# Vision block on one core: the weighing of the keys and the fills change places in TensorE's program from the third period on

## The reference

```
h = conv_involution(x)                       # per pixel: 16 hidden channels, relu, 9 filter taps;
                                             # out = sum over 9 taps of shifted x * tap; reshape (4, 4096, 64)
n = layernorm(h)
Q, K, V = n @ Wq + bq, n @ Wk + bk, n @ Wv + bv
h = h + softmax(Q @ K.T / sqrt(64)) @ V      # 4096 queries against 4096 keys, per image
n = layernorm(h)
idx = argmax(n @ router_w.T + router_b)      # one of 32 experts for each of 16384 tokens
t = relu(n @ W1[idx] + b1[idx])              # 64 -> 16
h = h + relu(t @ W2[idx] + b2[idx])          # 16 -> 64
```

## Time and profile before

| what | us |
|---|---|
| median of 3 runs (1106.17 to 1106.96) | 1106.2 |
| the profiled execution, its own time | 1105.74 |
| its span, first to last instruction | 1104.0 |
| TensorE (PE) busy | 1081.4 |
| PE weight loads busy | 531.2 |
| ScalarE busy | 575.2 |
| VectorE busy | 527.7 |
| one pass over 256 keys: scores, start to start of the next work | 1.72 |
| its weighing, likewise | 1.72 |

### The profile page before, as it was taken

The page is one execution under the profiler, slowest core; times in us unless marked ns, Lnnn a source line. Parts: engine busy times, 40 slices in busy tenths (PEclk is TensorE's granted clock), DMA queues, the critical chain, the costliest instruction groups (busy, mean ns, idle before and its releaser), DMA issues.

```text
span 1104.0 us, 28734 instructions
## 1 busy us (share of the span) xinstructions
PE 1081.4 (98%) x12492; PEld 531.2 (48%) x12492; DVE 527.7 (48%) x1039; ACT 575.2 (52%) x649; POOL 13.3 (1%) x44
## 2 busy tenths in 40 slices
PE   7799999999999999999999999999999999999997
PEld 4233333445454555435444454555555555555543
DVE  7888665436064553735546364564423131312305
ACT  2466666546555454645546454554645445464543
POOL 3100000000000000000000000000000000000000
PEclk9899999999999999999999999999999999999999
DMA  4847431113025141222313023240100101010000
GB/s 96 207 120 168 97 72 32 40 39 78 2 68 120 39 109 39 48 68 68 80 40 96 16 70 77 66 82 11 47 7 11 41 12 42 11 42 1 12 1 21
DMA packets 23377, 63.43 MB, mean 57 GB/s; under 512 B 4254, under 2 KB 8702, under 8 KB 22860
## 3 DMA queue, kind: packets, MB, share of 16 engines
q1 hardware_dynamic: 22364, 61.26, 23.3%
q10 hardware_dynamic: 880, 0.23, 0.1%
HBM read 52.87 MB, written 5.47 MB: 53 GB/s over the span
## 4 chain that ended last, share of the span: by engine, by line
PE 95%; DVE 1%; issue 1%; ACT 1%; DMA 1%; ACTq 0%; DVEq 0%; PEld 0%; PEldq 0%; SPq 0%
PE z_ps L787 40%; PE scores L776 38%; PE both L627 5%; PE both L758 4%; PE both L618 2%; PE both L766 1%; PE both L705 1%; PE both L724 1%; PE both L715 1%; DMA filter_ring<-filters 1%; PE both L750 0%; PE scores L627 0%; PE both L674 0%; DVE hres L1160 0%; PE z_ps L758 0%
## 5 line engine op out<-in xcount | busy, mean ns | idle before, releaser
L996 ACT ACTIVATE probs<-scores 128x1024 f32<-128x1024 f32 x512 | 496.4, 1021 | 470.7 <-PE scores L776 470.7
L776 PE MATMUL scores<-g_t,keys_t 64*64 64x512 f32 x4096 | 509.5, 591 | 1.5 <-ACT g_t L975 1.2
L787 PE MATMUL z_ps<-probs,keys 64*64 64x512 f32 x4096 | 506.8, 592 | 0.0
L776 PEld LDWEIGHTS scores<-g_t,keys_t 64*64 64x64 f32 x4096 | 210.9, 134 | 236.1 <-issue 230.1
L787 PEld LDWEIGHTS z_ps<-probs,keys 64*64 64x64 f32 x4096 | 196.4, 133 | 189.5 <-issue 178.6
L1220 DVE SCALAR_TENSOR_TENSOR hidden<-both,chosen 128x1024 f32<-128x1024 f32 x44 | 53.9, 1225 | 198.9 <-PE both L627 193.8
L1160 DVE TENSOR_TENSOR hres<-hres,tap_product 128x504 f32<-128x504 f32 (+1 forms) x128 | 88.1, 688 | 11.1 <-issue 0.9
L1148 DVE SCALAR_TENSOR_TENSOR tap_product<-filter_ring,w,xin 128x504 f32<-128x504 f32 (+1 forms) x117 | 87.0, 743 | 9.2 <-DMA filter_ring<-filters 5.5
L627 PE MATMUL both<-y_t,w 64*64 64x512 f32 x448 | 60.5, 589 | 0.0
L758 PE MATMUL both<-hidden,w 64*64 64x512 f32 x448 | 56.7, 592 | 0.0
L1261 DVE COPY o_sb<-both 128x512 f32<-128x512 f32 x14 | 9.7, 691 | 85.2 <-PE both L758 85.2
(11 more groups left out here) (162 smaller groups left out, 530.7 us busy)
## 6 DMA issues: line engine op xcount, KB each, us to landing
filter_ring<-filters SPq DMA_DIRECT2D x88, 384.0 KB, 5.4
chosen<-choices SPq DMA_DIRECT2D x44, 256.0 KB
out_dram<-out_sb SPq DMA_DIRECT2D x32, 128.0 KB, 2.4
xin<-x_dram SPq DMA_DIRECT2D x6, 528.0 KB, 9.3
g_t<-g_t SPq DMA_DIRECT2D x24, 128.0 KB, 6.2
hidden<-once_dram SPq DMA_DIRECT2D x1, 930.0 KB, 13.0
chosen<-filters SPq DMA_DIRECT2D x2, 384.0 KB, 7.3
choices<-onehot_t SPq DMA_DIRECT2D x22, 32.0 KB, 1.6
```

The lines of the kernel that those rows point to most:

```text
L776: last = T.matmul(scores[rows_of(h), c, r * 512:(r + 1) * 512], keys_t[rows_of(r), i // NQ % 2, k * 128 + 64 * h:k * 128 + 64 * h + 64], g ...
L787: last = T.matmul(z_ps[rows_of(c), h, :], keys[rows_of(h), i // NQ % 2, 2 * k + r, :], probs[rows_of(h), (2 * g + c) % RING, r * 512:(r + ...
L996: A.activation(probs[:, unit % RING, :], scores[:, c, :], ACT.Exp, scale=SCALE).then_inc(probs_ready, 1)
```

## The change

In `group(n, g, names)` the loop over the fills stood ahead of the weighing of group `g - 1`. Now this is so in periods 0 and 1 only; from period 2 on the fills stand behind it. The fills in group 0 already stood behind a weighing (that of the period before), and those of group 16 have none beside them: both stay as they are. So 150 fills move, those in groups 1 to 15 of the periods 2 to 15. The programs of ScalarE, VectorE, GpSimd and SyncE are unchanged.

```diff
                 at_once = n < 2 and g == HALF
                 if at_once:
                     usual_weigh(n, g - 1)
-                for full in names:
-                    fill(full)
+                if n < 2:
+                    for full in names:
+                        fill(full)
                 if n < BLOCKS and 0 < g < PAIRS and not at_once:
                     usual_weigh(n, g - 1)
+                if n > 1:
+                    for full in names:
+                        fill(full)
```

## The result

| kernel | median us | runs | lowest to highest |
|---|---|---|---|
| before | 1106.34 | 4 | 1106.17 to 1106.96 |
| after | 1125.85 | 4 | 1123.82 to 1127.43 |
| after, once more (with its own before of 1106.16) | 1126.63 | 5 | 1126.03 to 1127.66 |

The ratio is 1.0173 (95% interval 1.0158 to 1.0188), in the repetition 1.0187 (1.0171 to 1.0203). The change makes the kernel 19.5 us slower by the first comparison, 20.5 by the second. Forecast were 22.9 us and 1129.1. The direction and the mechanism were right. The size was too large: 1.0173 times the 1106.2 us of the start is 1125.3 us, just under the range of 1125.5 to 1134.0. The repetition (1.0187 times 1106.2 is 1126.9) lies inside it, so on which side of the bound a measurement falls is a matter of scatter; that the forecast was too large is not.

What follows compares the result with a forecast made beforehand. The prediction took TensorE, busy for 98% of the span, to bound the kernel. It added 18.9 + 1.5 + 2.5 = 22.9 us to the profiled 1105.74 us, and 0.5 for the median: 1129.1 us, range 1125.5 to 1134.0.

Steps and rivals of the forecast that it cites:

- What bounds the kernel, and that nothing can be gained: TensorE, busy 899.00 of 899.00 us from 151 to 1050 us, so no open wait that a new order could close.
- The moved fills cost nothing among themselves: Fills in successive groups shift alike by 1.72 us and drains keep 3.4 us of cover, so no cost.
- The bound of 0.03 us on each: Each of 150 moved fills may cost or save 0.03 us in its new slot, 4.5 us either way.
- `hid3` to `o2`, 11 x 1.72: Periods 4 to 14: `o2` stays, `hid3` comes up against it, TensorE waits for L1220; +18.9 us in all.
- the 2.61 us remain (fill, drain and the two signals): From start of `hid3` to start of `o2` stays 2.61 us, only 0.86 of them work; TensorE stands 1.75 us.
- The sign named for a wait under 1.5 us: If the 11 waits at `o2` are missing or shorter, the drain starts earlier behind a fill with nothing after it.
- `hid0@1` to `hid1@1`, 1.5: Period 2, once: `hid1` waits for ScalarE's L988 and starts at 227.27 instead of 225.81, +1.5 us.
- `z`, 12 x 0.21: Periods 4 to 15: first weighing waits 0.52 us for `z_sb`, partly regained in `fin`; +2.5 us in all.
- The lag: Behind `o2` two array quarters lag 0.31 us; the stall ahead of `fin` clears it; rival of no payback: 1132.8 us, 0.10.
- The clock: Rival: TensorE's clock falls at each of 11 new stalls, 17.6 us more, 1146.7 us; chance 0.04.
- The sum: 18.9 + 1.5 + 2.5 = 22.9 us over the whole kernel, giving 1129.1 us; within 2 us at chance 0.76.

## Why the prediction was right or wrong

- **What bounds the kernel, and that nothing can be gained**: right. TensorE's 899.00 of 899.00 us told that moved fills gain nothing, and 124 of them gained nothing. (The kernels without the bias gain by doing less work, not by the order.)
- **The moved fills cost nothing among themselves**: right, to 0.01 us in a period (65.15). The bound of 0.03 us on each was far wider than needed.
- **`hid3` to `o2`, 11 x 1.72**: right in place and kind, too large in size. It is 11 x 1.63. The step that failed is "the 2.61 us remain (fill, drain and the two signals)". The drain was done, and its weights could be loaded, 818.28 - 815.79 = 2.49 us behind the start of `hid3`; the last 0.12 us of the 2.61, taken for a signal, were the weighing. In before, `o2` did not start when the drain allowed it, but when the weighing's slot ended, at 816.65 + 1.72 = 818.37 of its 818.40. The true chain is 2.49 us (830.18 to 832.67 with only this group moved) and 2.46 with all moved, where the drain starts 0.03 us sooner. By the sum of the prediction 2.49 gives 2.49 - 0.86 - 0.03 = 1.60 us; the period grew by 1.63, and the last 0.03 were not traced. I read the weight load's wait as a sign of a cover with no margin; the run with a doubled drain shows a margin of 0.09 to 0.12. The sign named for a wait under 1.5 us, a drain that starts earlier, accounts for 0.03 us only.
- **`hid0@1` to `hid1@1`, 1.5**: it is 1.34. After, L992 ends at 226.39 + 1.02 = 227.41, and `hid1` starts at 227.47. The signal takes 0.06 us there, not the 0.15 taken from TensorE's wait in period 16.
- **`z`, 12 x 0.21**: it is 12 x 0.09. The lag is paid back as forecast. Up to the scores of group 2 the step costs 0.15 us, not 0.21: the signal is 0.10 us shorter than taken (0.05 instead of 0.15), but the weighing behind the stall holds TensorE for 1.77 us (830.12 to 831.89), not 1.72. Then 0.05 come back later, since the rest of the lag is gone that `fin` had not cleared.
- **The clock**: the rival is out. 11 stalls of 1.4 us left it at 1.00. The Trainium skill, "TensorE: Matmul & The Clock Gate", section "HAM oscillation — how this bites in real kernels", describes a kernel that is throttled anew at each pause, but its pauses are longer than these; the prediction gave the rule without that condition. With pauses of 1.4 us this trace does not show it.
- **The sum**: 22.9 forecast, 20.4 measured term by term. Of the 2.5 us, 1.0 are in the first term, 1.4 in `z` and 0.15 in `hid1`. Most of the 1.4 in `z` is 0.10 us of signal, times 12. The other 0.8 between 1129.1 and the first comparison's 1125.85 fit with the scatter of the start. The range reached 3.6 us below the forecast; the terms used up 2.5 of them, since all three erred the same way, two of them through one shared signal time.

## What to carry to other kernels

When an instruction moves in an in-order queue, look for the pairs whose second member stays: there alone cover is lost, and the loss is the chain (work, drain, signals) less the work. Do not take that chain from the distance at which the second member starts now if other work ends at the same moment; that distance is only an upper bound. What showed the chain's own length here was the earliest trace of readiness, the weight load at 2.49 us. And where one signal time goes into several terms, their errors add up rather than cancel.

## What the runs showed of the hardware that was not expected

- A matmul that had waited started 0.05 us after the end of the VectorE instruction that it waited for (832.34 + 1.23 = 833.57 to 833.62), and 0.06 us after ScalarE's (227.41 to 227.47). In period 16 the signal took 0.15 us, before (1075.39 to 1075.54) and after (1095.85 to 1096.00). Why the two differ was not tried.
- Two bf16 matmuls more in each of two of the array's four quarters (the four of L750 in `o2`) cost a period in which TensorE never rests 0.43 us, though matmuls of L758 already ran beside them (818.41 in before). The lag is carried through 5.15 us of scores and weighing (821.89 to 827.04 in before, records of 2.30 us; in the kernel without the bias 817.54 to 822.69, records of 1.93) and comes due mostly at the first short matmuls.
- Waits of the weight load in the list of waits cost nothing in 22 places of one kernel: 6.4 us in 11 places at L627 and as much at L750, while its period was that of before (65.15 us).
